# A cross-attention and expert kernel: one folded normalization, key projections placed in waits, memsets in pieces

## What is computed

```
# layer 0: one head of width 128
x = x + softmax((ln(x) Wq + bq)(ctx Wk + bk)^T / sqrt(128)) (ctx Wv + bv)
# layer 0 experts: one of 8, H = 32, chosen by argmax
xn = ln(x)                      # the kernel's normalization ahead of the router
xhat = (xn - mean(xn)) * rsqrt(var(xn) + 1e-5)
x = x + (gelu((xhat * s_e + b_e) W1_e + b1_e) W2_e + b2_e)   for e = argmax(xn Wg^T)
# layer 1: eight heads of width 64
x = x + concat_h softmax(ln(x) Wq_h (ctx Wk_h)^T / 8) (ctx Wv_h) Wo + bo
# layer 1 experts: 4 of 32 by a grouped top-k, and a shared one
```

## Time and profile before

| | |
|---|---|
| runs before | 1486.12, 1483.55, 1484.18 us; median 1484.18 |
| profiled execution | 1484.28 us, its span 1482.5 us |
| TensorE busy | 1396.7 us, 94% of the span |
| VectorE busy | 1111.0 us, 75% |
| GpSimd busy | 938.7 us, 63% |
| ScalarE busy | 807.6 us, 54% |

### The profile page before, as it was taken

How to read it: one execution, slowest core, us unless ns; L and a number is a source line. 1 busy time by engine, 2 the same in 40 slices (tenths; PEclk the granted TensorE clock), 3 DMA queues, 4 the chain that set the end, 5 groups by cost and what they waited for, 6 DMA issues and landing times.

```text
span 1482.5 us, 20192 instructions
## 1 busy us (share of the span) xinstructions
PE 1396.7 (94%) x6199; PEld 791.9 (53%) x6199; DVE 1111.0 (75%) x1518; ACT 807.6 (54%) x1625; POOL 938.7 (63%) x512
## 2 busy tenths in 40 slices
PE   4989996878999999999999999999999999997798
PEld 2867774533455545554555555555555555554465
DVE  6976567479779688778868877887887886766755
ACT  3768884232556556555655655665555555454232
POOL 5001115022689888978988898898898899885110
PEclk9999998565899999999999999999999999998799
DMA  6640000040000200020020011002002000000011
GB/s 158 208 134 17 17 17 7 1 91 2 1 1 1 49 1 1 1 49 1 1 48 1 1 28 22 0 1 49 0 1 45 1 1 1 1 1 13 19 37 39
DMA packets 77371, 39.42 MB, mean 27 GB/s; under 512 B 62047, under 2 KB 70000, under 8 KB 77002
## 3 DMA queue, kind: packets, MB, share of 16 engines
q1 hardware_dynamic: 77290, 38.36, 10.5%
HBM read 24.66 MB, written 13.68 MB: 26 GB/s over the span
## 4 chain that ended last, share of the span: by engine, by line
PE 86%; DVE 7%; DMA 3%; ACT 2%; issue 1%; POOL 0%; SPq 0%; ACTq 0%; DVEq 0%; POOLq 0%
PE ps L1348 24%; PE ps L1335 14%; PE ps L1336 12%; PE ps L1301 9%; PE ps L1288 3%; DMA v_scratch<-v_stage 2%; DVE chunk_max L921 2%; PE ps L1491 2%; PE ps L1191 2%; PE ps L1192 2%; PE ps L1193 2%; PE ps L1182 2%; PE ps L1180 2%; PE ps L1181 2%; PE ps L1280 1%
## 5 line engine op out<-in xcount | busy, mean ns | idle before, releaser
L506 POOL TENSOR_TENSOR psums<-psums,probs 126x1024 f32<-126x1024 f32 (+1 forms) x392 | 820.9, 2094 | 123.4 <-ACT probs L689 74.5
L689 ACT ACTIVATE probs<-ps 126x512 f32<-126x512 f32 (+1 forms) x816 | 416.4, 617 | 273.4 <-PE ps L1336 267.5
L921 DVE TENSOR_REDUCE chunk_max<-ps 128x2 f32<-128x1008 f32 (+1 forms) x416 | 472.9, 1180 | 79.5 <-PE ps L1301 77.9
L1348 PE MATMUL ps<-probs,v_mem 126*64 126x512 f32 (+1 forms) x1632 | 389.7, 598 | 0.0
L1335 PE MATMUL ps<-q_heads,ring 128*126 128x512 f32 (+1 forms) x816 | 342.9, 420 | 1.2
L1336 PE MATMUL ps<-q_low,ring 128*126 128x512 f32 (+1 forms) x816 | 322.5, 395 | 0.0
L974 DVE TENSOR_TENSOR xn<-xn,probs 126x512 f32<-126x512 f32 x126 | 230.6, 1830 | 29.9 <-ACT probs L689 25.6
L648 ACT CAST ring<-ps 64x252 fp32r<-64x252 f32 (+1 forms) x356 | 128.3, 360 | 135.9 <-PE ps L1288 132.8
L1348 PEld LDWEIGHTS ps<-probs,v_mem 126*64 126x64 f32 (+1 forms) x1632 | 111.5, 136 | 165.4 <-issue 121.2
L1335 PEld LDWEIGHTS ps<-q_heads,ring 128*126 128x126 f32 (+1 forms) x816 | 152.1, 186 | 88.8 <-issue 44.2
L1301 PE MATMUL ps<-ring,q_heads 64*128 64x504 f32 (+1 forms) x416 | 168.5, 477 | 15.8 <-DVE chunk_max L921 6.7
(11 more groups left out here) (200 smaller groups left out, 1456.7 us busy)
## 6 DMA issues: line engine op xcount, KB each, us to landing
v_scratch<-v_stage SPq DMA_DIRECT2D x51, 252.0 KB
v_mem<-v_scratch SPq DMA_DIRECT2D x8, 1606.5 KB
ctx_mem<-in_ctx_t SPq DMA_DIRECT2D x3, 803.2 KB, 9.3
vslot<-in_ctx_rows SPq DMA_DIRECT2D x51, 47.2 KB
pair_w<-in_f_pairs SPq DMA_DIRECT2D x17, 128.0 KB, 2.1
pair_w<-in_f_pairs SPq DMA_DIRECT2D x17, 65.0 KB, 1.8
x_tok<-in_x SPq DMA_DIRECT2D x1, 512.0 KB, 3.6
wo<-in_c_wo SPq DMA_DIRECT2D x1, 512.0 KB
```

What stands on the lines that cost most here:

```text
L506: pool.tensor_tensor(sums[0:r, 0:width], sums[0:r, 0:width], probs[0:r, n % PROBS, 0:width], ALU.add).then_inc(c_sum, 1)
L689: act.activation(probs[0:r, n % PROBS, cols(half)], ps[0:r, score_bank(t, half), :], ACT.Exp, scale=float(HD) ** -0.5).then_inc(c_exped, 1)
L921: dve.tensor_reduce(chunk_max[:, h % 2, i:i + 2, c], ps[:, banks[0]:banks[1] + 1, 0:group_tiles(c) * KT], AX, ALU.max).then_inc(c_reduced, 1)
L1348: ins = pe.matmul(ps[half * HD:(half + 1) * HD, B_ACC, :], v_tiles[0:r, h % 2, t, :], probs[0:r, n % PROBS, cols(half)], start=(t == 0), s ...
```

## The change

Start: `neg_ident` and the identity's load get a semaphore of their own (`in_id`) and VectorE no longer waits for them ahead of the normalization; VectorE fills the row of ones of `keys_hl` as its first instruction; the two other memsets of `keys_hl` move on GpSimd behind the copies of the queries; ScalarE does one square root of a constant as its first instruction; the products of the key weights go to banks 6 and 7; the first maxima wait for neither `a_qlo` nor `a_wvs`, which the value products now wait for.

Experts of layer 0: normalization 2 goes, and normalization 1 takes sqrt((1 + eps) v + eps^2) instead, so that router and experts read the same `xn_t`. Nine key projections are taken out of the maxima: 0 to 2 (banks 4 and 5 in turn) stand ahead of the first transposes, 3 to 5 behind hidden products 0 and 1, 6 to 8 behind the output products. ScalarE's copies of them (`k_first`) stand at the places that the diff shows. The mask is copied in two halves, behind the second Gelu. The products with b2 come first, and those with W2 follow as each quarter of the hidden values has been masked. The addition to `x_tok` is in halves. Banks are dealt out anew.

Key stage: the memsets of the ring are cut into pieces, a pair for each slot, and each pair stands ahead of that slot's remainder on GpSimd; the addition of `bo` stands ahead of slot 9. The remaining projections 9 to 14 stand at the second step of the first six groups.

```diff
+EARLY = (3, 6, 9)
+B_LOGITS, B_HIDDEN, B_SPREAD, B_MASK = 0, (1, 2, 3, 6), (5, 1, 2, 3), (7, 0)
...
+def key_bank(g):
+
+    return FIRST_KP + g % 2 if g < EARLY[0] else FIRST_KP
...
-            pool.memset(f32(keys_hl[CD:CD + 1, :, 0, :]), 1.0).then_inc(a_rows, 1)
-            pool.wait_ge(a_rows, 5)
-            pool.memset(f32(keys_hl[CD:P, :, 1, :]), 0.0).then_inc(a_rows, 1)
-            pool.wait_ge(a_rows, 6)
-            pool.memset(f32(keys_hl[CD:CD + 1, TILES - 1, 1, PAD_AT:KT]), 1.0).then_inc(a_rows, 1)
...
+            pool.memset(f32(keys_hl[CD:P, :, 1, :]), 0.0).then_inc(a_rows, 1)
+            pool.wait_ge(a_rows, 5)
+            pool.memset(f32(keys_hl[CD:CD + 1, TILES - 1, 1, PAD_AT:KT]), 1.0).then_inc(a_rows, 1)
...
+            pool.memset(f32(q_low[0:HD, :, :]), 0.0).then_inc(q_zero, 1)
             for g in range(AHEAD):
                 n = group_tiles(g % GROUPS_H)
                 if g:
                     pool.wait_ge(c_klo_first, g)
+                if g == EARLY[-1]:
+                    pool.wait_ge(ln_out, 3 * TT)
+                    pool.wait_ge(in_c, 48)
+                    pool.tensor_tensor(x_tok[:, :, :], x_tok[:, :, :], bo1[:, :].unsqueeze(1).to_broadcast([P, TT, D]),
+                                       ALU.add).then_inc(c_bo, 1)
+                    pool.wait_ge(c_bo, 1)
+                if g == AHEAD - 1:
+                    pool.memset(f32(ring[0:HD, g:RING, :, 1, :]), 0.0).then_inc(ring_rows, 1)
+                    pool.wait_ge(ring_rows, 2 * g + 1)
+                    pool.memset(f32(ring[0:TT, g:RING, :, 1, :]), 1.0).then_inc(ring_rows, 1)
+                else:
+                    pool.memset(f32(ring[0:HD, g, :, 1, :]), 0.0).then_inc(ring_rows, 1)
+                    pool.wait_ge(ring_rows, 2 * g + 1)
+                    pool.memset(f32(ring[0:TT, g, :, 1, :]), 1.0).then_inc(ring_rows, 1)
+                pool.wait_ge(ring_rows, 2 * g + 2)
                 pool.wait_ge(c_kfull, g + 1)
                 pool.tensor_tensor(ring[HD:P, g, 0:n, 1, :], k_full[:, g % 2, 0:n, :], f32(ring[HD:P, g, 0:n, 0, :]),
                                    ALU.subtract).then_inc(c_klo_first, 1)
...
+                if twice:
+
+                    act.activation(std[:, :], mean_var[:, :, 1], ACT.Sqrt, bias=eps2_col[:, :],
+                                   scale=1.0 + EPS).then_inc(ln_std, 1)
+                else:
+                    act.activation(std[:, :], mean_var[:, :, 1], ACT.Sqrt, bias=eps_col[:, :]).then_inc(ln_std, 1)
...
+            act.wait_ge(consts, 4)
+            act.activation(first_std[:, :], zero_col[:, :], ACT.Sqrt, bias=eps_col[:, :])
             std_of(0)
...
+            def k_first(g):
+                n = group_tiles(g % GROUPS_H)
+                act.wait_ge(c_kp, g + 1)
+                act.copy(ring[:, g, 0:n, 0, :],
+                         ps[:, key_bank(g), 0:n * KT].rearrange("p (n k) -> p n k", k=KT)).then_inc(c_khi, 1)
+                if g >= 2:
+                    act.wait_ge(c_klo_first, g - 1)
+                act.copy(k_full[:, g % 2, 0:n, :],
+                         ps[HD:P, key_bank(g), 0:n * KT].rearrange("p (n k) -> p n k", k=KT)).then_inc(c_kfull, 1)
+
+            for j in range(CH):
+                act.wait_ge(a_vout[j], 16 * CHUNKS)
+            k_first(0)
+            std_of(1, twice=True)
+            for g in range(1, EARLY[0]):
+                k_first(g)
             turned(1, xn_t)
-            std_of(2)
-            turned(2, xn_t)
+            for g in range(EARLY[0], EARLY[1]):
+                k_first(g)
             act.wait_ge(f_biassb, 1)
             for n in range(2 * G0):
                 g, half = n // 2, n % 2
+                if n == 2:
+                    act.wait_ge(f_pe, PE_MASK)
+                    for part in range(2):
+                        ins = act.copy(mask_t[:, cols(part)], ps[0:E0, B_MASK[part], :])
+                    ins.then_inc(f_masktsb, 1)
                 act.wait_ge(f_pe, PE_HIDDEN[n])
-                act.activation(hid0[:, g, cols(half)], ps[:, 2 + n, :], ACT.Gelu, bias=hb0[:, g:g + 1]).then_inc(f_gelu, 1)
-                if n == 0:
-                    act.wait_ge(f_pe, PE_MASK)
-                    act.copy(halves(mask_t), ps[0:E0, 0:2, :]).then_inc(f_masktsb, 1)
-
-
-            std_of(3)
-            turned(3, xn_t)
+                act.activation(hid0[:, g, cols(half)], ps[:, B_HIDDEN[n], :], ACT.Gelu, bias=hb0[:, g:g + 1]).then_inc(f_gelu, 1)
+            for g in range(EARLY[1], EARLY[2] - 1):
+                k_first(g)
+            std_of(2)
+            k_first(EARLY[2] - 1)
+            turned(2, xn_t)
...
-            for g in range(AHEAD):
-                n = group_tiles(g % GROUPS_H)
-                k_hi(g, FIRST_KP)
-                if g >= 2:
-                    act.wait_ge(c_klo_first, g - 1)
-                act.copy(k_full[:, g % 2, 0:n, :],
-                         ps[HD:P, FIRST_KP, 0:n * KT].rearrange("p (n k) -> p n k", k=KT)).then_inc(c_kfull, 1)
-                if g in (2, 3):
-                    q_hi(1, g - 2, B_AUX)
+            for g in range(EARLY[2], AHEAD):
+                k_first(g)
+                if g in (EARLY[2] + 1, EARLY[2] + 2):
+                    q_hi(1, g - EARLY[2] - 1, B_AUX)
...
-            dve.wait_ge(in_x, 32)
-            dve.tensor_scalar(neg_ident[:, :], ident[:, :], -1.0, None, ALU.mult).then_inc(neg_ready, 1)
+            dve.memset(f32(keys_hl[CD:CD + 1, :, 0, :]), 1.0).then_inc(a_ones, 1)
+            dve.wait_ge(in_x, 16)
             layernorm(0, x_tok, xn)
...
+            dve.wait_ge(in_id, 16)
+            dve.tensor_scalar(neg_ident[:, :], ident[:, :], -1.0, None, ALU.mult).then_inc(neg_ready, 1)
...
-            dve.wait_ge(ln_out, 2 * TT)
-            layernorm(2, xn, xn2)
             dve.wait_ge(f_pe, PE_LOGITS)
-            dve.tensor_copy(lg0, ps[:, 4, 0:TT * E0]).then_inc(f_step, 1)
-            turned(2, xn_t)
...
+            for half in range(2):
+                ins = dve.tensor_tensor(x_tok[:, half * 4:half * 4 + 4, :],
+                                        ps[:, B_MASK[half], :].rearrange("p (t d) -> p t d", d=D),
+                                        x_tok[:, half * 4:half * 4 + 4, :], ALU.add)
+            ins.then_inc(f_x, 1)
...
-            pe.wait_ge(a_rows, 7)
-            pe.wait_ge(a_qlo, 1)
-            pe.wait_ge(a_wvs, 2)
...
+                        if g == 0 and j == 0:
+                            pe.wait_ge(a_wvs, 2)
+                        if g == 0 and j == 2:
+                            pe.wait_ge(a_qlo, 1)
...
+            def k_proj(g):
+                h, c = divmod(g, GROUPS_H)
+                if c == 0:
+                    pe.wait_ge(c_wk[h % 2], 16 * (h // 2 + 1))
+                if g == 1:
+                    pe.wait_ge(f_biassb, 1)
+                if g >= 1 and key_bank(g) == key_bank(g - 1):
+                    pe.wait_ge(c_kfull, g)
+                elif g >= 2:
+                    pe.wait_ge(c_kfull, g - 1)
+                at, width = c * GT * KT, group_tiles(c) * KT
+                pe.matmul(ps[:, key_bank(g), 0:width], wk1[:, h % 2, :], ctx_f[:, at:at + width], start=True,
+                          stop=True).then_inc(c_kp, 1)
+
+
             pe.wait_ge(f_w, 2)
-            pe.wait_ge(consts, 3)
+            pe.wait_ge(consts, 1)
             for g in range(G0):
-                ins = pe.matmul(ps[:, 5, g:g + 1], w1b[:, tile_cols(g)], ones[:, 0:1], start=True, stop=True)
+                ins = pe.matmul(ps[:, B_AUX, g:g + 1], w1b[:, tile_cols(g)], ones[:, 0:1], start=True, stop=True)
             ins.then_inc(f_pe, 1)
+            for g in range(EARLY[0]):
+                k_proj(g)
             turn(1, xn, 1)
             turned(1)
             pe.wait_ge(in_f0, 16 * 9)
+            pe.wait_ge(a_x, 1)
             for t in range(TT):
-                ins = pe.matmul(ps[:, 4, t * E0:(t + 1) * E0], xn_t[:, tile_cols(t)], wgt, start=True, stop=True)
+                ins = pe.matmul(ps[:, B_LOGITS, t * E0:(t + 1) * E0], xn_t[:, tile_cols(t)], wgt, start=True, stop=True)
             ins.then_inc(f_pe, 1)
-            turn(2, xn2, 2)
-            turned(2)
-            pe.wait_ge(a_x, 1)
-            pe.wait_ge(f_step, 1)
-            pe.wait_ge(f_biassb, 1)
 
             def hidden(n):
                 g, half = n // 2, n % 2
-                pe.matmul(ps[:, 2 + n, :], w1s[:, tile_cols(g)], xn_t[:, cols(half)], start=True, stop=True).then_inc(f_pe, 1)
+                pe.matmul(ps[:, B_HIDDEN[n], :], w1s[:, tile_cols(g)], xn_t[:, cols(half)], start=True, stop=True).then_inc(f_pe, 1)
 
             for n in range(2):
                 hidden(n)
+            for g in range(EARLY[0], EARLY[1]):
+                k_proj(g)
             pe.wait_ge(f_mask, 1)
             for t in range(TT):
-                ins = pe.transpose(ps[0:E0, t // 4, tile_cols(t % 4)], mask0[:, t, :], ident[:, :])
```

(70 more changed lines are left out.)

70 lines of the change are left out of this document (25 added, 45 removed).

## The result

| | before | after |
|---|---|---|
| median of the timed runs, us | 1485.72 (1483.55 to 1488.95, 7 runs) | 1479.81 (1478.89 to 1484.09, 7 runs) |
| ratio, 95% interval | | 0.9964 [0.9948, 0.9979] |
| profiled execution, us | 1484.28 | 1484.09 |

A forecast was written before the change was run, and what follows sets the result against it. TensorE bounds 86% of the chain, mostly the unchanged heads; only the first 29 us and 246 to 376 us can move. -2.3 + 3.0 + 5.3 - 0.6 - 1.2 - 1.2 = +3.0, with rounding 1487.5 us, range 1478 to 1491.

The forecast's parts named there:

- The order of the output products changes, not their number: 48 passes in 15.0 us: Output products of the first expert layer: length unchanged at 0.31 us a pass; 7.5 us gained only as a 2.4 GHz bound.
- start: Kernel start to the first reduction: 2.3 us gained, bounds 1 and 4, with reductions starting at 27.0 us.
- memsets in pieces, to the logits: Layer one's normalization: subtracts take 4.1 us beside short GpSimd memsets, logits start 5.5 us earlier, bounds 4.5 and 7.3.
- second normalization: Expert layer, logits to hidden products: 3.56 us instead of 6.23 without the second normalization, 2.7 us gained.
- projections 3 to 5, hidden start to transposes: Key projections ahead of the mask's transposes, all in bank 4, push them back: 8.0 us lost, bounds 4.5 and 9.0.
- transposes to first spread: Mask transposes to first spread: ScalarE's copies, Gelus and table load, and hidden products 2 and 3, lose 2.4 us, bounds 1.5 and 2.9.
- first spread to output: Spreads take 5.3 us, between 3.69 and 6.9 by clock, 1.7 lost; bias products fill a 0.86 us pause, 0.9 gained.
- output's end to query product: Next normalization, behind projections 6 to 8, their copies and a table load: 5.3 us lost, bounds 2.4 and 6.
- to the first reduction, maxima, tail: Query product to the end of the key stage: 0.6, 1.2 and 1.2 us gained, from fewer copies and projections there.
- Rounds of 2.5 us there: Projection starts behind hidden product 0 and the output were to be 3.4 us apart; 2.5 would disprove the forecast.
- Rival A: The clock stays up, so projection rounds behind hidden products and output are short: 5.4 us gained, 1478.9; chance 0.26.
- The memset forecast: VectorE's one-row memset of 6426 elements at the start: about 5.7 us (3.5 or 6.7 at other rates), ending at 6.5 us.

The follow-up runs named there:

- experiment 5: Kernel before, old order of output products, both operands of the b2 product padded with zeros to 128 rows: 1481.15 us in its one run.
- experiments 6 to 8: Changed kernel with key projections moved later: 3 to 8 one stage on (0.9885), 6 to 8 into the maxima (0.9928), 3 to 8 into the maxima, ring memsets long (0.9914).
- experiments 6 and 7: Changed kernel: first, projections 3 to 5 behind the output and 6 to 8 in the maxima, 1468.46 us; second, only 6 to 8 into the maxima, 1474.44 us.
- experiment 2: Changed kernel with the output products back in the old order, behind one wait for all masked tiles: 1485.99 us, ratio 0.9986 to the kernel before.
- experiment 1: Kernel before with only the output products reordered, all b2 first, then W2 group by group over the tiles: 1480.39 us, ratio 0.9949.
- experiment 3: Kernel before with all b2 products first, then the two W2 products of each tile behind each other: 1481.05 us in its one run.
- experiments 2, 4 and 11: First: see experiment 2. Second: kernel before, W2, W2, b2 in turn, each to another tile, 1484.41 us. Third: kernel before with the changed start alone, 1482.87 us.
- (3, 3, 3): Changed kernel with key projections 3 to 8 moved into the maxima loop and ring memsets from group 3 on in one long piece: 1473.73 us, ratio 0.9914.

## Why the prediction was wrong

The step that failed is "The order of the output products changes, not their number: 48 passes in 15.0 us". It was priced at nothing but a pause of 0.9. The runs show 5.3 us in the profiled pair and 7.6 us (4.7 to 10.4) on its own, of which the 16 changes of height account for 4.7. The bound of 7.5 us gained that stands beside the step was for a doubled clock, and the clock was 0.50 until 289 us in the changed kernel. I had divided 15.0 by 48 and called 0.31 us the length of a pass at the lower clock, where at a granted clock of 0.50 a pass of this shape takes 0.21 (1.28 / 6, experiment 5). I noted that TensorE "never pauses there": the ends of products are modelled, so PE showed 14.00 of 14 us, and the weight loads stood beside it, unread: 10.63 of 14 us, or 2.93 of 4.00 in the earlier trace rows itself.

Term by term, profiled pair unless said otherwise:

| step | predicted | measured |
|---|---|---|
| start | -2.3 | -3.0 (0.9980 [0.9968, 0.9993], run alone) |
| memsets in pieces, to the logits | -5.5 | -5.8 |
| second normalization | -2.7 | -2.8 |
| projections 3 to 5, hidden start to transposes | +8.0 | +7.2 (10.59 in place of 3.38) |
| transposes to first spread | +2.4 | +2.3 |
| first spread to output | +1.7 - 0.9 | -0.2 |
| output products | 0 | -5.3 |
| output's end to query product | +5.3 | +3.1 |
| to the first reduction, maxima, tail | -3.0 | -3.1 (-0.25, -1.7, -1.1) |

The measured terms from the second on add up to -4.6 us, the forecast's to +5.3. The -1.7 of the maxima is inside the spread told with experiments 6 to 8. The start has the right size by luck: the reductions were to begin at 27.0 us and began at 28.27, since VectorE's remainders ended at 25.64 us, at the late end of what the text gave (24 to 25.6), and the three short steps behind them took 2.7 us. Seven of the nine have the right sign, among them that projections in the waits cost more than they give (10.2 and 4.3 us by experiments 6 and 7). Those that are too large by 0.8 and 2.2 us share a cause: I priced rounds at 3.41 us (less 1 us for one of those ahead of the transposes), and they took 2.81 and 2.39 ahead of the transposes (granted clock 0.81 and 0.85 there) and 2.28 and 2.38 behind the output (1.00). "Rounds of 2.5 us there", the text said, would prove it wrong. With these and the spreads as measured (another 1.0) the forecast had been 1483.5: no change, which is what the change is without the new order (0.9986, experiment 2). The output products alone carry it past that. The 6.9 us for spreads at the lower clock stood on no row, and no run has such spreads: the longest, in experiment 2, took 4.98 us at a granted clock of 0.73. Rival A had nearly the time (1478.9) and the short rounds, but not the mechanism: it left the output at its old length and took what that gives from the other stages.

On the clock, the prediction had it against rival A that by 284 us it had fallen with hardly a pause, which is the 0.50 of the output products in the earlier trace rows. Without the changes of height the clock does rise before they end: to 1.00 from 288 us on in experiment 1, to 0.65 between 288 and 290 us in experiment 3, to 0.93 between 285 and 289 in experiment 5, to 0.57 between 288 and 290 in the changed kernel. With them it is at 0.50 until they end (before, experiments 2, 4 and 11). What I took for a dense stretch had its weight loads idle for 0.22 us ahead of each change; whether that kept the clock down no run shows.

The memset forecast was right in size (5.7 us predicted, 5.41 measured, that is 0.84 ns an element), but it started at 2.16 us and so ended at 7.57, not at 6.5. The 3.5 and 6.7 us beside the 5.7 stood on no row.

## What to carry to other kernels

Before you call a run of products dense, divide its time by its passes and compare with passes of the same shape elsewhere in the profile: here 0.31 us a pass in place of 0.21 came from changes between tall and short stationary operands, and those could be grouped, or padded away. Work moved into a wait of an engine is free only if its whole chain (bank, copies, and the table load that stands behind them) ends before the wait does; here three projections cost 10.2 us in one wait and 4.3 in another, and in the loop that VectorE paces too little to tell from the spread between profiles. When a variant comes out as you forecast, look at the stage all the same: (3, 3, 3) hit its range and hid 7 us.
